# Cross-attention for 64 batches: one output projection and one sum of heads move to the end of a step

## The chip, the cores and the metric

The kernel runs on one core of one Trainium2 chip. The core has a matrix engine (PE, with its weight loads shown apart as PEld), a vector engine (DVE), an activation engine (ACT), a general engine (POOL) and a queue that issues transfers (SP). The metric is the time of one execution on the device, in microseconds (us); lower is better.

## The reference

For each of 64 batches there are 256 queries of width 320 and 77 context rows of width 512. Of these 69 are text and 8 belong to an image prompt, each with its own key and value weights. There are 20 heads of width 16. Text and image part have softmaxes of their own, and their results are added:

```
q = split_heads(x @ w_q)
out_text = sdpa(q, split_heads(text @ w_k), split_heads(text @ w_v))
out_ip   = sdpa(q, split_heads(ip @ w_k_ip), split_heads(ip @ w_v_ip), mask=box_mask)
out = (merge_heads(out_text) + merge_heads(out_ip)) @ w_out + b_out + x
```

`sdpa` is softmax(q k^T / 4 + mask) v. The mask of the image part comes from four boxes on a 16 x 16 grid of queries.

## The kernel before

A first part (to about 240 us) projects keys and values of all batches and stores them in device memory. The second part does the attention. It is a software pipeline over batches: step n works on batch a = n+1 (transposing x, projecting q, maxima of the scores), b = n (scores and exponentials), c = n-1 (sums over keys, output of queries 0 to 127) and d = n-2 (output of queries 128 to 255). All engines run the same steps. Four steps, then a hardware loop whose body holds six steps (so there is a loop-back every six steps), then the last steps.

Each step has 7 positions s = 0 to 6. Nothing reorders the work: every engine executes its instructions in the order in which its `step` function writes them, and the engines meet at semaphores. PE's order is at L963 to L993, ACT's at L999 to L1055, DVE's at L1066 to L1184, POOL's at L1190 to L1211. The work that matters here:

- `scores(b, s)`: matmuls of 2 of the 13 tiles of keys into one of three banks `ps_s`; ACT makes two exponentials of them, and POOL a remainder (`prob_lo`).
- `max_scores(a, m)`, m = 0 to 9, into two banks `ps_m`; DVE's `maxima(m)` adds the mask and reduces them into `stats` (L1097, L1100, and for m = 8 and 9 also L1104). max_scores(m) waits for maxima(m-2).
- `stats_transpose(a)` (L879): two PE transposes of `stats` into `ps_b`. It waits for the last reduction of maxima(9). ACT copies the result into `q_hi_extra` (L1052, and L1053 with four copies); the lower-half matmuls of the next step's scores (L905) need it. `x_transpose(a, 1)` waits for L1053 because it writes `ps_b`.
- `x_transpose(a, 0)` (L828): the first PE work of a step, into `ps_a`. Its wait on `s_yr` asks for the `finish(c, 0)` of the step before.
- `attn_transpose`, `project_out(c, 0)` (L951, a bias matmul L959 and 8 matmuls at L852 into `ps_a`), then DVE's `finish(c, 0)` (L1135), which adds x into `y`. SP stores `y`.
- `sum_heads(c, u)`, u = 0 to 5 (L909): matmuls of the probabilities with the spread values into the single bank `ps_o`. DVE's `invert(u)` (L1110) and `norm(u)` (L1118) empty it; POOL adds the two parts into `attn` (L1208). sum_heads(u) waits for norm(u-1). u = 5, a group of 4 heads, is the last.
- `spread_values` (L1145): three DVE multiplications at s = 4, 5, 6.
- At the start of the next step ACT and DVE split the transposed x (`x_hi`, `x_lo`), which `project(a, 0)` (PE, L852 into `ps_b`) waits for.

Of the kernel before, what the change touches and what calls it, by code (L numbers as in the profile page):

```python
# [37 lines left out]
UNITS = NT * 3  # L38
# [93 lines left out]
def xattn_kernel(nc, x, ctx, bbox, w_q, w_k, w_v, w_k_ip, w_v_ip, w_out, b_out,  # L132
# [6 lines left out]
    with ctx_stack:  # L139
# [513 lines left out]
        with ExitStack() as st:  # L653
# [99 lines left out]
            with nc.Block() as block:  # L753
# [71 lines left out]
                def _(pe):  # L825
# [53 lines left out]
                    def stats_transpose(b, n):  # L879
                        pe.wait_ge(s_ip, at(b, NT, NT))  # L880

                        if n is None or n >= 1:
                            pe.wait_ge(s_alo, at(b, NT, 1 - 2 * NT))
                        else:
                            pe.wait_ge(s_qlo, at(b, QUADS, 4))
                        for t in range(NT):
                            last = nc.tensor.transpose(ps_b[:, t * P:(t + 1) * P], stats[:, t, :], ident[:])  # L887
                        last.then_inc(s_et, 1)
# [62 lines left out]
                    def project_out(b, t, A):  # L951
                        pe.wait_ge(s_alo, at(b, NT, t + 1))

                        if t == 0 and A:
                            pe.wait_ge(s_qlo, at(b, QUADS, QUADS * 2 + 5))
                        elif t == 0:
                            wait(pe, s_yr, b, NT, 0)
                        c = slice(t * P, (t + 1) * P)
                        mm(ps_a[:, 0:D], ones[:], bias[:], start=True, stop=False)  # L959
                        split_product(ps_a[:, 0:D], lambda k: aT[0][:, k, c], lambda k: aT[1][:, k, c], aT2[:, c],  # L960
                                      wo, slice(0, D), False, False).then_inc(s_op, 1)

                    def step(pe, b, n):  # L963
                        A, Bs, Cs, Ds = has(n)
                        a, c = off(b, 1), off(b, -1)
                        d = off(b, -2)
                        for s in range(PAIRS):
                            if A and s == 0:
                                x_transpose(a, 0, n)
                            if Bs:  # L970
                                scores(b, s)
                            if A and s == 0:
                                x_transpose(a, 1, n)
                            if Ds and s == 1:
                                attn_transpose(d, 1, A, n)
                            if Ds and s == 2:
                                project_out(d, 1, A)
                            if A and s in (1, 2, 3):
                                project(a, s - 1)
                            if A and MAXIMA[s]:  # L980
                                max_scores(a, MAXIMA[s][0])
                            if Cs:
                                if s == 4:
                                    attn_transpose(c, 0, A, n)
                                if s == 5:
                                    project_out(c, 0, A)
                                if s < UNITS:
                                    sum_heads(c, s)
                            if A:
                                for m in MAXIMA[s][1:]:  # L990
                                    max_scores(a, m)
                        if A:
                            stats_transpose(a, n)  # L993

                    sched(pe, step)

                @block.scalar
# [62 lines left out]
                def _(dve):  # L1060
# [5 lines left out]
                    def step(dve, b, n):  # L1066
                        A, Bs, Cs, Ds = has(n)
# [59 lines left out]
                        def finish(c, t):  # L1127
                            dve.wait_ge(s_op, at(c, NT, t + 1))
                            if t == 0:
                                dve.wait_ge(s_xk[par(c)], nth(c, 16))  # L1130

                                reg = c[0] is not None
                                if reg or c[1] >= 2:
                                    dve.wait_ge(s_y[par(c)], nth(c, 32, -32))
                            nc.vector.tensor_tensor(y[par(c)][:, t, :], ps_a[:, 0:D], x_keep[par(c)][:, t, :],  # L1135
                                                    ALU.add).then_inc(s_yr, 1)

                        def spread_values(g):

                            if g == 0:  # L1140
                                dve.wait_ge(s_vals[par(b)], nth(b, 16 * NVDMA))
                                wait(dve, s_pv, b, UNITS, -UNITS)
                            v = values[par(b)][:].rearrange("p (t n c) -> p t n c", t=TILES, c=SLOT)
                            t = slice(GTILE[g], GTILE[g] + GTILES[g])
                            nc.vector.tensor_tensor(  # L1145
                                v[:, t, :, 2:SLOT],
                                raw_v[par(b)][:].rearrange("p t (o c) -> p t o c", o=1)[:, t]
                                .broadcast_to([P, GTILES[g], SLOTS, 3 * DH]),
                                own_rows[:].rearrange("p t (n c) -> p t n c", n=SLOTS)[:, t], ALU.mult).then_inc(s_vx, 1)
# [7 lines left out]
                        for s in range(PAIRS):  # L1157
                            if A and s == 0:
                                x_lo(0)
                                x_lo(1)  # L1160
                            if Ds and s == 1:
                                a_lo(d, 1)
                            if Ds and s == 2:
                                finish(d, 1)
                            if A and MAXIMA[s]:
                                maxima(MAXIMA[s][0])
                            if A and s in (1, 2, 3):
                                q_lo(s - 1)
                            if Cs and s == 4:
                                a_lo(c, 0)  # L1170
                            if Cs and s == 5:
                                finish(c, 0)
                            if Cs and s < UNITS:
                                invert(s)
                            if A:
                                for m in MAXIMA[s][1:2]:
                                    maxima(m)
                            if Cs and s < UNITS:
                                norm(s)
                            if A:  # L1180
                                for m in MAXIMA[s][2:]:
                                    maxima(m)
                            if Bs and s in (4, 5, 6):
                                spread_values(s - 4)  # L1184

                    sched(dve, step)

# [48 lines left out]
```

## Time and profile before

| What | Value |
|---|---|
| median of 3 runs (lowest, highest) | 1598.76 us (1596.06, 1602.39) |
| the profiled execution, its time | 1604.02 us |
| the profiled execution, its span in the trace | 1602.1 us |
| PE busy | 1385.2 us (86%) |
| PEld busy | 1266.7 us (79%) |
| DVE busy | 1173.1 us (73%) |
| ACT busy | 848.4 us (53%) |
| POOL busy | 806.3 us (50%) |
| mean granted PE clock | 0.959 |

The span covers one execution, from its first instruction to its last. Busy time is the time in which an engine executes; it says nothing of whether the others wait for it. The granted clock is 1.0 at 2.4 GHz and 0.5 at 1.2 GHz, the two levels at which PE runs.

### The profile page before, as it was taken

What the parts mean: (1) busy time and instruction counts of PE and PEld (TensorE: products, weight loads), DVE (VectorE), ACT (ScalarE), POOL (GpSimd) and SP (SyncE); (2) the same over time, 40 slices, a digit from 0 to 9 for tenths busy, and PEclk for the clock granted to TensorE, in tenths of its full rate; (3) what the DMA queues carried; (4) which work ended last, traced back from release to release, by engine and by line L of the source; (5) the groups of instructions that cost most, each with busy time, mean ns of one, the idle gap of its engine ahead of it and who ended that gap; (6) DMA issues with size and microseconds to landing.
All of it is one profiled execution on the core that took longest, in us unless ns stands there. A gap on an engine that the chain in (4) does not pass through costs nothing.

```text
span 1602.1 us, 48578 instructions
## 1 busy us (share of the span) xinstructions
PE 1385.2 (86%) x15736; PEld 1266.7 (79%) x15736; DVE 1173.1 (73%) x3602; ACT 848.4 (53%) x2064; POOL 806.3 (50%) x1038
## 2 busy tenths in 40 slices
PE   6778775899989989989998998998998998999997
PEld 5778774788878878878887887887887888888886
DVE  5368443788878877877887886887887886888885
ACT  3344432555555555555555555555554555555553
POOL 0132220555555555555555555555555555555554
PEclk9899995999999999999999999999999999999998
DMA  5788994343333443433433333433433333444331
GB/s 136 112 199 171 187 168 88 84 93 94 92 74 89 93 95 88 93 93 87 93 93 86 93 93 71 94 92 88 93 93 91 94 93 85 93 94 93 94 76 37
DMA packets 361215, 159.25 MB, mean 99 GB/s; under 512 B 298417, under 2 KB 350514, under 8 KB 359666
## 3 DMA queue, kind: packets, MB, share of 16 engines
q1 hardware_dynamic: 355826, 134.83, 37.3%
q10 hardware_dynamic: 5120, 20.98, 6.3%
q8 instruction: 152, 2.49, 0.7%
q14 instruction: 117, 0.96, 0.2%
HBM read 91.69 MB, written 43.05 MB: 84 GB/s over the span
## 4 chain that ended last, share of the span: by engine, by line
PE 42%; DVE 14%; issue 14%; ACT 10%; ACTq 2%; DVEq 1%; POOL 1%; DMA 0%; POOLq 0%; SPq 0%
PE ps_o L928 9%; PE ps_a L852 9%; PE ps_b L852 8%; PE ps_m L876 5%; PE ps_s L899 4%; PE ps_s L905 4%; ACT prob_hi L1037 3%; DVE values L1145 3%; ACT xT_hi L1007 2%; DVE y L1135 2%; PE ps_b L887 2%; DVE stats L1104 2%; ACT aT_hi L1025 2%; ACTq L1018 2%; DVE inv L1110 1%
## 5 line engine op out<-in xcount | busy, mean ns | idle before, releaser
L1197 POOL TENSOR_TENSOR prob_lo<-prob,prob_hi 128x512 f16<-128x512 f32 (+1 forms) x448 | 488.9, 1091 | 169.5 <-ACT prob_hi L1037 169.3
L1208 POOL TENSOR_TENSOR attn<-heads 128x128 f32<-128x128 f32 (+1 forms) x512 | 271.9, 541 | 440.0 <-DVE heads L1118 440.0
L1036 ACT ACTIVATE prob<-ps_s 128x512 f32<-128x512 f32 (+1 forms) x448 | 254.0, 567 | 388.6 <-PE ps_s L905 379.9
L928 PE MATMUL ps_o<-values,prob_hi 128*128 128x64 bf16 (+7 forms) x4992 | 311.3, 196 | 3.8 <-DVE values L1145 1.8
L928 PE MATMUL ps_o<-values,prob_lo 128*128 128x68 bf16 (+7 forms) x3328 | 300.2, 196 | 0.0
L928 PEld LDWEIGHTS ps_o<-values,prob_hi 128*128 128x128 f16 x4992 | 268.8, 99 | 25.8 <-DVE values L1145 2.0
L1100 DVE TENSOR_REDUCE stats<-ps_m 128x4 f32<-128x276 f32 x640 | 277.0, 433 | 0.0
L899 PE MATMUL ps_s<-q_hi_lo,keys 128*128 128x256 f32 x960 | 260.3, 305 | 0.0
L1037 ACT ACTIVATE prob_hi<-ps_s 128x512 f16<-128x512 f32 (+1 forms) x448 | 251.4, 561 | 0.0
L905 PE MATMUL ps_s<-q_hi_extra,keys 128*128 128x256 f32 x960 | 246.1, 292 | 0.9 <-ACT q_hi_extra L1052 0.3
L876 PE MATMUL ps_m<-keys,q_hi_lo 128*128 128x308 f32 x640 | 219.2, 360 | 12.7 <-DVE stats L1100 4.8
L928 PEld LDWEIGHTS ps_o<-values,prob_lo 128*128 128x128 f16 x3328 | 217.0, 99 | 0.0
L905 PEld LDWEIGHTS ps_s<-q_hi_extra,keys 128*128 128x128 f32 x960 | 177.6, 195 | 11.4 <-ACT q_hi_extra L1052 11.1
L899 PEld LDWEIGHTS ps_s<-q_hi_lo,keys 128*128 128x128 f32 x960 | 178.4, 196 | 0.0
L1118 DVE TENSOR_TENSOR heads<-ps_o,inv 128x256 f32<-128x256 f32 (+1 forms) x384 | 143.3, 373 | 15.1 <-DVE inv L1110 0.5
L876 PEld LDWEIGHTS ps_m<-keys,q_hi_lo 128*128 128x128 f32 x640 | 116.3, 190 | 41.4 <-DVE stats L1100 33.0
L1014 ACT CAST q_hi_lo<-ps_b 64x256 fp32r<-64x256 f32 x256 | 94.1, 368 | 100.7 <-PE ps_b L852 97.4
L1097 DVE TENSOR_TENSOR ip_masked<-ps_m,stats 128x32 f32<-128x32 f32 x640 | 105.1, 164 | 54.9 <-PE ps_m L876 48.8
L1145 DVE TENSOR_TENSOR values<-raw_v,own_rows 128x1200 bf16<-128x1200 bf16 (+1 forms) x192 | 136.3, 737 | 0.0
L1087 DVE TENSOR_TENSOR q_hi_lo<-ps_b,q_hi_lo 64x256 fp32r<-64x256 f32 x256 | 108.1, 422 | 14.9 <-ACT q_hi_lo L1014 7.0
L1110 DVE RECIPROCAL inv<-ps_o 128x16 f32<-128x16 f32 (+1 forms) x384 | 91.6, 239 | 15.3 <-PE ps_o L928 5.6
L852 PE MATMUL ps_b<-xT_hi,wq_hi 128*128 128x256 f32 x256 | 80.3, 314 | 17.3 <-DVE xT L1074 15.4
(165 smaller groups left out, 3032.5 us busy)
## 6 DMA issues: line engine op xcount, KB each, us to landing
x_in<-in_x_dram SPq DMA_DIRECT2D x64, 320.0 KB, 3.3
q_hi_extra<-q_hi_lo ACTq DMA_DIRECT2D x64, 320.0 KB, 3.3
x_keep<-in_x_dram SPq DMA_DIRECT2D x64, 320.0 KB, 3.2
out_dram<-y SPq DMA_DIRECT2D x128, 160.0 KB, 1.8
k_scratch<-k_stage SPq DMA_DIRECT2D x16, 770.0 KB, 5.8
keys<-k_scratch SPq DMA_DIRECT2D x256, 48.1 KB, 2.0
ctx_in<-in_ctx_dram SPq DMA_DIRECT2D x64, 128.0 KB, 3.1
v_scratch<-v_stage SPq DMA_DIRECT2D x64, 120.0 KB, 5.5
```

Source lines behind the costliest of these rows:

```text
L852: last = mm(ps, ww if swap else a, a if swap else ww, start=first and n == 0, stop=n == len(terms) - 1)
L876: mm(ps_m[n % 2][:, 0:QUAD], q_hl[par(b)][:, h4, t * P:(t + 1) * P], keys[:, third(b), 0, h4, KOFF:KOFF + QUAD], start=True, stop=True).th ...
L899: mm(ps, keys[:, n, 0, quad, c:c + P], q_hl[q][:, quad, :], start=i == 0, stop=False)
L905: last = mm(ps, keys[:, n, 1, quad, c:c + P], q_ex[q][:, quad, :], start=False, stop=i == len(QPARTS[t]) - 1)
L928: last = mm(o[:, :, oo:oo + w], stat, v[:, :, a:a + w], start=first, stop=False, skip_group_check=True)
L1036: nc.scalar.activation(prob[:, s, 0:w], ps_s[RING[s]][:, 0:w], ACT.Exp)
L1037: nc.scalar.activation(prob_hi[par(b)][:, s, 0:w], ps_s[RING[s]][:, 0:w], ACT.Exp).then_inc(s_hi, 1)
L1100: nc.vector.tensor_reduce(stats[:, t, R_MT + 4 * h4:R_MT + 4 * h4 + 4], ps[:, :, 0:T], AX.X, ALU.max).then_inc(s_mx, 1)
L1118: nc.vector.tensor_tensor(heads[u % 2][:, 0:ns, :], o[:, :, 1:17], inv[:, 0:ns].rearrange("p (n o) -> p n o", o=1).broadcast_to([P, ns, DH ...
L1145: nc.vector.tensor_tensor(v[:, t, :, 2:SLOT], raw_v[par(b)][:].rearrange("p t (o c) -> p t o c", o=1)[:, t] .broadcast_to([P, GTILES[g], S ...
L1197: nc.gpsimd.tensor_tensor(prob_lo[par(b)][:, s, 0:w], prob[:, s, 0:w], prob_hi[par(b)][:, s, 0:w], ALU.subtract).then_inc(s_lo, 1)
L1208: last = nc.gpsimd.tensor_tensor(attn[:, t, c0:c0 + nh * DH].rearrange("p (h c) -> p h c", c=DH), hv[:, :, 0, :], hv[:, :, 1, :], ALU.add)
```

## The change

The pieces `project_out(c, 0)` and `sum_heads(c, 5)` leave position 5 of a step on PE and stand behind `stats_transpose(a)`, at the very end of the step. DVE's matching pieces `finish(c, 0)`, `invert(5)` and `norm(5)` leave position 5 and stand behind the last `spread_values`. ACT, POOL and SP keep their orders. No instruction is added or left out.

```diff
--- before.py
+++ after.py
@@ -982,15 +982,16 @@
                             if Cs:
                                 if s == 4:
                                     attn_transpose(c, 0, A, n)
-                                if s == 5:
-                                    project_out(c, 0, A)
-                                if s < UNITS:
+                                if s < UNITS - 1:
                                     sum_heads(c, s)
                             if A:
                                 for m in MAXIMA[s][1:]:
                                     max_scores(a, m)
                         if A:
                             stats_transpose(a, n)
+                        if Cs:
+                            project_out(c, 0, A)
+                            sum_heads(c, UNITS - 1)
 
                     sched(pe, step)
 
@@ -1168,20 +1169,22 @@
                                 q_lo(s - 1)
                             if Cs and s == 4:
                                 a_lo(c, 0)
-                            if Cs and s == 5:
-                                finish(c, 0)
-                            if Cs and s < UNITS:
+                            if Cs and s < UNITS - 1:
                                 invert(s)
                             if A:
                                 for m in MAXIMA[s][1:2]:
                                     maxima(m)
-                            if Cs and s < UNITS:
+                            if Cs and s < UNITS - 1:
                                 norm(s)
                             if A:
                                 for m in MAXIMA[s][2:]:
                                     maxima(m)
                             if Bs and s in (4, 5, 6):
                                 spread_values(s - 4)
+                        if Cs:
+                            finish(c, 0)
+                            invert(UNITS - 1)
+                            norm(UNITS - 1)
 
                     sched(dve, step)
```

The changed file has one line more above its DVE part, so a DVE line of before has a number one higher there.

PE, where position 5 of one of the first steps ends (later steps have the same order): a `-` is a row of before, a `+` one of the changed order. `L876` is max_scores(9), `L899` and `L905` scores(6), `L887` stats_transpose, `L959` and the first `L852` the start of project_out(c, 0).

```order
 L899 MATMUL ps_s<-q_hi_lo,keys 128x256
 L905 MATMUL ps_s<-q_hi_extra,keys 128x256
-L876 MATMUL ps_m<-keys,q_hi_lo 128x308
+L876 MATMUL ps_m<-keys,q_hi_lo 128x308 x2
+L899 MATMUL ps_s<-q_hi_lo,keys 128x256
+L905 MATMUL ps_s<-q_hi_extra,keys 128x256
+L887 MATMUL ps_b<-ident,stats 128x128 x2
 L959 MATMUL ps_a<-bias,ones 128x320
 L852 MATMUL ps_a<-wo_hi,aT_hi 128x320
```

max_scores(9), scores(6) and the transposes of the statistics now come ahead of project_out. The other end of the same piece, behind the last matmuls of sum_heads(5) (`L928`), where the next step's x_transpose (`L841`) follows:

```order
 L928 MATMUL ps_o<-values,prob_lo 128x34
 L928 MATMUL ps_o<-values,prob_lo 128x2x16
-L876 MATMUL ps_m<-keys,q_hi_lo 128x308
-L899 MATMUL ps_s<-q_hi_lo,keys 128x256
-L905 MATMUL ps_s<-q_hi_extra,keys 128x256
-L887 MATMUL ps_b<-ident,stats 128x128 x2
 L841 MATMUL ps_a<-ident,x_in 128x128 x2
 L843 MATMUL ps_a<-ident,x_in 128x128
```

The next step's first transposes used to follow the transposes of the statistics, and now follow sum_heads(5).

DVE, from maxima(8) to the first instruction of the next step, before (`L1135` is finish, `L1110` invert, `L1118` norm, `L1145` spread_values, `L1154` the next step's copy of the mask):

```order
L1097 TENSOR_TENSOR ip_masked<-ps_m,stats 128x32
L1100 TENSOR_REDUCE stats<-ps_m 128x4
L1104 TENSOR_REDUCE stats<-ip_masked 128x20
L1135 TENSOR_TENSOR y<-ps_a,x_keep 128x320
L1110 RECIPROCAL inv<-ps_o 128x8
L1097 TENSOR_TENSOR ip_masked<-ps_m,stats 128x32
L1100 TENSOR_REDUCE stats<-ps_m 128x4
L1104 TENSOR_REDUCE stats<-ip_masked 128x20
L1118 TENSOR_TENSOR heads<-ps_o,inv 128x128
L1145 TENSOR_TENSOR values<-raw_v,own_rows 128x25x48
L1145 TENSOR_TENSOR values<-raw_v,own_rows 128x15x48
L1154 COPY stats<-mask 128x2x8
```

And the same stretch as changed (line numbers one higher):

```order
L1098 TENSOR_TENSOR ip_masked<-ps_m,stats 128x32
L1101 TENSOR_REDUCE stats<-ps_m 128x4
L1105 TENSOR_REDUCE stats<-ip_masked 128x20
L1098 TENSOR_TENSOR ip_masked<-ps_m,stats 128x32
L1101 TENSOR_REDUCE stats<-ps_m 128x4
L1105 TENSOR_REDUCE stats<-ip_masked 128x20
L1146 TENSOR_TENSOR values<-raw_v,own_rows 128x25x48
L1146 TENSOR_TENSOR values<-raw_v,own_rows 128x15x48
L1136 TENSOR_TENSOR y<-ps_a,x_keep 128x320
L1111 RECIPROCAL inv<-ps_o 128x8
L1119 TENSOR_TENSOR heads<-ps_o,inv 128x128
L1155 COPY stats<-mask 128x2x8
```

maxima(9) now follows maxima(8) directly, and finish, invert and norm stand behind both spreads.

## Rows read from the trace of the kernel before

**Rows 1.** Stretches, all engines: us, busy us per engine, PEclk, DMA share, GB/s

```profile
1031.00:1051.00 20.00, 18.27 (x226) 16.63 (x226) 16.26 (x54) 11.82 (x29) 11.71 (x15) 1.00 0.40 93
...
1091.00:1116.50 25.50, 20.67 (x226) 19.12 (x226) 16.26 (x55) 11.81 (x29) 11.76 (x15) 0.87 0.32 76
```

**Rows 2.** Waits: engine, line, releaser: us in total, times, longest us

```profile
PE ps_b L887 <- DVE stats L1104: 67.2, 64, 2.1
...
PE ps_a L841 <- issue: 28.2, 8, 3.9
...
DVE stats L1154 <- issue: 11.1, 8, 1.6
```

**Rows 3.** PE, timeline, one step's end: start, us, what [idle before <- releaser]

```profile
1007.71 0.41 PE L959 MATMUL ps_a<-bias,ones 128*128 128x320 f32 x1
...
1009.14 0.25 PE L928 MATMUL ps_o<-values,prob_hi 128*128 128x51 bf16 x3
...
1009.60 0.39 PE L876 MATMUL ps_m<-keys,q_hi_lo 128*128 128x308 f32 x1
1009.83 0.28 PE L899 MATMUL ps_s<-q_hi_lo,keys 128*128 128x256 f32 x1
1009.95 0.28 PE L905 MATMUL ps_s<-q_hi_extra,keys 128*128 128x256 f32 x1
1011.24 0.44 PE L887 MATMUL ps_b<-ident,stats 128*128 128x128 f32 x2 [1.01 <-DVE stats L1104]
1011.51 0.38 PE L841 MATMUL ps_a<-ident,x_in 128*128 128x128 f32 x2
...
1011.76 0.36 PE L899 MATMUL ps_s<-q_hi_lo,keys 128*128 128x256 f32 x1
...
1013.05 0.44 PE L841 MATMUL ps_b<-ident,x_in 128*128 128x128 f32 x2 [0.29 <-ACT q_hi_extra L1053]
...
1015.24 0.27 PE L949 MATMUL ps_a<-ident,attn 128*128 128x128 f32 x1
1015.77 0.39 PE L852 MATMUL ps_b<-xT_hi,wq_hi 128*128 128x256 f32 x1 [0.25 <-DVE xT L1074]
```

**Rows 4.** DVE, timeline, the same step's end

```profile
1007.91 0.43 DVE L1100 TENSOR_REDUCE stats<-ps_m 128x4 f32<-128x276 f32 x1
...
1009.96 0.48 DVE L1135 TENSOR_TENSOR y<-ps_a,x_keep 128x320 f32<-128x320 f32 x1
...
1010.47 0.13 DVE L1097 TENSOR_TENSOR ip_masked<-ps_m,stats 128x32 f32<-128x32 f32 x1
...
1010.88 0.30 DVE L1104 TENSOR_REDUCE stats<-ip_masked 128x20 f32<-128x160 f32 x1
1011.10 0.28 DVE L1118 TENSOR_TENSOR heads<-ps_o,inv 128x128 f32<-128x128 f32 x1
1011.30 1.34 DVE L1145 TENSOR_TENSOR values<-raw_v,own_rows 128x1200 bf16<-128x1200 bf16 x2
```

**Rows 5.** ACT, timeline, just behind it

```profile
1013.02 0.37 ACT L1007 CAST xT_hi<-ps_a 128x256 fp32r<-128x256 f32 x1
...
1013.45 0.60 ACT L1036 ACTIVATE prob<-ps_s 128x512 f32<-128x512 f32 x1
```

**Rows 6.** POOL, timeline, the two adds of the last sum

```profile
1011.46 1.36 POOL L1208 TENSOR_TENSOR attn<-heads 128x64 f32<-128x64 f32 x2 [0.67 <-DVE heads L1118]
```

**Rows 7.** PE, timeline behind a loop-back

```profile
1095.02 0.69 PE L841 MATMUL ps_a<-ident,x_in 128*128 128x128 f32 x2 [3.43 <-issue]
...
1100.83 0.50 PE L852 MATMUL ps_b<-xT_hi,wq_hi 128*128 128x256 f32 x1
```

**Rows 8.** PE, timeline: first and last of six idle stretches of 1.6 to 2.1 us

```profile
93.89 0.87 PE L464 MATMUL ps_t<-ident,ctx_in 128*128 128x128 f32 x4 [1.81 <-DMA ctx_in<-in_ctx_dram]
...
1582.04 0.25 PE L928 MATMUL ps_o<-values,prob_hi 128*128 128x51 bf16 x3 [1.79 <-DVE values L1145]
```

**Rows 9.** Stretch behind the last of them, columns as in rows 1

```profile
1582.00:1586.00 4.00, 3.68 (x54) 3.31 (x55) 1.41 (x5) 0.53 (x2) 1.25 (x3) 0.57 0.02 4
```

## The prediction

> **What bounds the kernel now.** I read the time by stretches first, then the waits, then the timelines of one step. A step in the loop takes 20.0 us with PE busy for 18.3 of them at the full clock, and a step behind a loop-back takes 25.5 us, with a mean granted clock of 0.87 [rows 1]. PE is the busiest engine, so the question is where it is not busy. The list of waits answers: in each of 64 steps PE waits for DVE's last reduction before the transposes of the statistics, 67.2 us in all or 1.05 us each, and at each of 8 loop-backs it waits 3.5 us for nothing that the profile shows [rows 2]. The timeline of one step adds two short waits: 0.29 us until ACT has read `ps_b` empty, and 0.25 us for xT_lo [rows 3]. Call the start of the statistics' transposes T (1011.24 in the rows). Two chains meet there:
>
> - Up to T the end is set by DVE. From 1007.91 its rows follow each other without a gap: maxima, norm, a spread, maxima(8), y, an inversion, maxima(9) [rows 4]. PE is through with scores(6) at 1010.23 and stands still until T [rows 3].
> - From T to the first matmul of project(a, 0) at 1015.77 are 4.53 us. Here ACT is in line: it copies the statistics, then x_hi(0) from 1013.02, the exponentials from 1013.45, x_hi(1), and DVE's x_lo(1); from the exponentials' start to project are 2.32 us [rows 3, 5].
>
> From project to scores(4) of the step PE has work without a stop, and the change touches nothing there.
>
> **The change part by part.** Nothing is added or removed; three things move. I place them on the rows of the same step.
>
> *DVE ahead of T.* y, the inversion and their gaps stand between maxima(8) and maxima(9): 1010.47 - 1009.96 = 0.51 us [rows 4]. They go, so maxima(9) ends 0.51 us earlier and T comes at 1010.73. What is late next is the same chain of DVE.
>
> *PE ahead of T.* The moved matmuls last 1009.14 - 1007.71 = 1.43 us (project_out) and 1009.60 - 1009.14 = 0.46 us (sum_heads(5)), together 1.89 us [rows 3]. They ran while DVE worked towards T, so there they cost nothing. Without them PE has max_scores(9), which must wait for maxima(7) (its row ends at 1008.34 [rows 4]), then scores(6), and is done by about 1009.0. It then waits until 1010.73. The wait of 1.0 us becomes 1.7 us, with a new one of about 0.55 us shortly ahead of it. That is the heart of the forecast: PE had cover to give under DVE's chain, and the change takes it away.
>
> *Behind T.* The 1.89 us now stand between the transposes (0.27) and the next step. The two matmul groups hide ACT's copies, so the 0.29 us wait goes, and a wait of 0.2 us in the first scores. But x_transpose(0) may not start before y is made. project_out ends at T + 1.70, its last result 0.2 later; DVE has finished both spreads (1.34 us [rows 4]) by then and waits for it; y takes 0.48; so x_transpose(0) starts at T + 2.44, not at T + 2.16. Its three transposes reach ACT 0.49 later, x_hi(0) takes 0.43 until the exponentials can start [rows 5], which is T + 3.40; scores(0), four matmuls 0.12 apart [rows 3], is ready just before. With 2.32 more, project starts at T + 5.72. PE alone needs, from T + 2.44, 0.25 for the transposes, 0.5 for scores(0), and 1015.51 - 1013.05 = 2.46 for x_transpose(1) up to the end of attn_transpose [rows 3]: T + 5.65. Both limits are nearly equal. The stretch is 5.72 instead of 4.53 us: +1.19.
>
> *What is queued behind.* On DVE the inversion, norm(5) and the next step's mask copy stand behind y; they end by T + 3.2, before x_lo(0) can start. POOL's two adds, 1.36 us at most [rows 6], wait for norm(5) and then hold up one prob_lo; attn is ready at about T + 4.4, and attn_transpose comes at T + 5.0: hidden. SP stores y some 3 us later (y ends at T + 2.4, and at T - 0.8 before [rows 4]) and loads values behind it, for a step that is two away: hidden. If these covers fail the price is up to 1 us a step.
>
> *Sum at the full clock:* -0.51 + 1.19 = +0.68 us a step. 62 steps have both moved pieces and a next step, 8 of them end in a loop-back, so 54 x 0.68 = +37 us.
>
> *The clock.* This is the unknown. PE's longer stall may cost it the clock. In this trace there are six idle stretches of PE between 1.6 and 2.1 us that began at full clock, and behind four of them the clock fell; the last was 1.79 us long and the mean clock of the next 4 us was 0.57 [rows 8, 9]. At half clock for a time z in these 4 us the mean is 1 - z/8, so the low lasted about 3.4 us. The waits of 1.0 us in the steady steps never brought it down: the clock there is 1.00 [rows 1]. The new stall of 1.7 us, with 0.55 us of idleness near it, lies in the range of the six. Price of one fall: behind the loop-back the stretch from x_transpose(0) to project took 1100.83 - 1095.02 = 5.81 us at half clock [rows 7], against 0.25 + 0.5 + 2.46 = 3.2 us, so work runs 1.8 times as long; 3.4 us of it put PE back by 1.5 us, of which the small waits above take 0.2: 1.3 us. Bounds: 0 where it never falls, 1.3 a step where it falls in each. By the rows, 4 of 6; the second idle stretch close by speaks for more; I take three in four, 0.98 us a step: 54 x 0.98 = +53 us.
>
> The Trainium skill speaks against this. "TensorE: Matmul & The Clock Gate", section "Why this matters for your kernels", asks only that idle gaps between bursts of matmuls stay below a length that is well above the stall that I expect. By that rule the clock would hold and the sum would be that of the first rival. The trace does not agree: a gap of 1.79 us was enough at 1582.
>
> *The loop-back.* In 8 steps the stall of 3.5 us came straight behind T's transposes and hid ACT's work. If it starts only when the moved work is done, such a step grows by 1.89 - 0.51 = 1.4 us; if PE's queue takes the moved matmuls while the next code is fetched, it shrinks by 0.5 at best, less what is left: -0.3. DVE's rows speak for overlap: at the same loop-backs DVE, with 1.34 us of spreads in its queue, stood idle for only 1.4 us where PE stood 3.5 [rows 2, 4]. I take +0.6: 8 x 0.6 = +5 us. The clock is low behind loop-backs anyway.
>
> The skill's table at the head of the same page gives TensorE a queue of 64 instructions, into which the 24 moved matmuls and their weight loads would fit; by that the lower end holds and the sum is 7 us less. No row shows PE's queue at a loop-back with work in it.
>
> **Sum.** 37 + 53 + 5 = +95 us on the profiled execution's own time of 1604.0 us (its span is 1602.1): 1699 us. The median of the runs shown, 1598.8, is 5.3 lower, so I forecast 1694 us.
>
> **The rivals.**
>
> *The clock holds.* Then 37 + 5 = +42 us: 1641 us. For it: 20.0 us steps with a 1.0 us wait and further small ones keep the full clock, and two of the six gaps did no harm, one of them 2.04 us long. Against: the other four.
>
> *The clock falls in every step.* 54 x (0.68 + 1.3) + 8 x 1.4 = +118 us: 1717 us. It is the upper part of my own case.
>
> *Faster: T moves further ahead than I place it.* If DVE reached maxima(9) earlier than 1010.73, because its work before T shortens when PE and POOL press less on it, the moved matmuls would fill waits that are worth 1.0 + 0.29 + 0.2 + 0.25 us. It decides at T = 1010.05, where the step's length is unchanged. At T = 1009.5 the step gains 0.55 us: 54 x 0.55 = -30 us: 1569 us. Against it: DVE's rows before T have no gap to give back, and the only instructions removed from them are those 0.51 us.
>
> *No effect.* The new waits replace the old ones one for one, 1599 us. It would need T near 1010.05 as well.
>
> **How the numbers follow.** The clock falls in most steps: 0.58, and this is the forecast, with a range of its own of 1665 to 1722. The clock holds: 0.27. Some mixture or a hidden cost between the other cases, slower by more than 0.5%: 0.04. No effect within 0.5% (8 us, about what a measurement of this kernel can tell from no change): 0.04. Faster: 0.07. So faster 0.07, same 0.04, slower 0.89. The range has to take in the rival with the clock held, with some room below (1630), and the case of a fall in each step above (1725).
>
> **What would show it.** In the changed profile: (1) PE's wait before L887 on DVE's L1105 grows from 1.05 to about 1.7 us a step, and waits before the max_scores on DVE's L1101 grow by about 0.5 us a step; (2) ACT's L1053 no longer releases PE; x_transpose(0) waits for DVE's y (L1136) for some tenths; (3) from T to the first matmul of project are about 5.7 us in a step at full clock; (4) the mean granted clock of the span falls from 0.96 to about 0.92 (three quarters of 54 lows of 3.4 us at half clock in 1699 us are 0.04), with lows inside steady steps and not only behind loop-backs; (5) steady steps of 20.7 us where the clock holds and near 22 where it falls. I am wrong if T comes ahead of 1010.05 on the scale of these rows, or if PE's stall before T isn't longer than before; the clock term alone is wrong if lows stay confined to the loop-backs.

## The result, and the profile after

| | before | changed |
|---|---|---|
| median of 4 runs (lowest, highest) | 1598.8 us (1596.06, 1602.39) | 1685.13 us (1683.01, 1690.06) |
| profiled execution, span | 1602.1 us | 1681.2 us |
| mean granted PE clock over the span | 0.959 | 0.934 |

The changed kernel is slower: the ratio of its time to that of before is 1.054, 95% interval 1.051 to 1.057. The forecast was 1694 us with a range of 1630 to 1725.

The page of the changed kernel, first part and clock row (tenths of full speed in 40 slices), and below them the clock row of before. The work is the same, but low slices now stand all over the span:

```profile
PE 1405.9 (84%) x15736; PEld 1298.2 (77%) x15736; DVE 1179.0 (70%) x3602; ACT 851.0 (51%) x2064; POOL 759.2 (45%) x1038
...
PEclk9889977999999989989899998998998998989998
```

```profile
PEclk9899995999999999999999999999999999999998
```

Three stretches of the changed kernel, each one step long, columns as in [rows 1]: a step at full clock, a step with a fall of the clock, a step with a loop-back.

```profile
449.31:470.11 20.80, 18.04 (x227) 16.57 (x227) 16.30 (x54) 11.88 (x29) 10.95 (x16) 1.00 0.38 90
1470.81:1492.76 21.95, 19.43 (x226) 17.93 (x227) 16.33 (x54) 11.92 (x29) 10.94 (x16) 0.91 0.36 85
603.72:630.14 26.42, 21.34 (x226) 19.89 (x227) 16.55 (x54) 11.82 (x29) 11.01 (x16) 0.81 0.32 74
```

A plain step takes 20.8 us where it took 20.0, and the step at 1470.81 holds a clock fall far from any loop-back (mean 0.91); between 300 us and the last T no step of before held one, apart from those with a loop-back. The loop-back's step takes 26.4 us at a mean clock of 0.81, against 25.5 and 0.87 [rows 1].

The waits of the changed kernel that answer [rows 2], with two new ones (us in total, times, longest us):

```profile
PE ps_b L887 <- DVE stats L1105: 112.7, 64, 2.1
...
PE ps_m L876 <- DVE stats L1101: 39.0, 77, 0.7
...
DVE stats L1155 <- issue: 24.0, 8, 3.2
...
PE ps_a L841 <- issue: 22.2, 8, 3.7
...
PE ps_a L841 <- DVE y L1136: 10.7, 38, 0.4
```

PE's wait before the statistics' transposes has grown from 67.2 to 112.7 us, it now waits for maxima ahead of max_scores (39.0 us, 4.8 before) and for y ahead of the next x_transpose (10.7 us). At the loop-backs PE's wait has shrunk, from 28.2 to 22.2 us, and DVE's has grown from 11.1 to 24.0.

PE's timeline at one step's end, the answer to [rows 3]. T, the start of L887, is here 407.72:

```profile
405.34 0.41 PE L876 MATMUL ps_m<-keys,q_hi_lo 128*128 128x308 f32 x1 [0.56 <-DVE stats L1101]
...
407.72 0.44 PE L887 MATMUL ps_b<-ident,stats 128*128 128x128 f32 x2 [1.74 <-DVE stats L1105]
407.91 0.39 PE L959 MATMUL ps_a<-bias,ones 128*128 128x320 f32 x1
...
409.32 0.25 PE L928 MATMUL ps_o<-values,prob_hi 128*128 128x51 bf16 x3
...
410.15 0.41 PE L841 MATMUL ps_a<-ident,x_in 128*128 128x128 f32 x2 [0.21 <-DVE y L1136]
...
413.51 0.39 PE L852 MATMUL ps_b<-xT_hi,wq_hi 128*128 128x256 f32 x1
```

DVE in the same place, the answer to [rows 4] (numbers one higher: L1098, L1105 maxima, L1146 spreads, L1136 y):

```profile
406.23 0.18 DVE L1098 TENSOR_TENSOR ip_masked<-ps_m,stats 128x32 f32<-128x32 f32 x1
...
407.35 0.31 DVE L1105 TENSOR_REDUCE stats<-ip_masked 128x20 f32<-128x160 f32 x1
407.58 1.24 DVE L1146 TENSOR_TENSOR values<-raw_v,own_rows 128x1200 bf16<-128x1200 bf16 x2
409.51 0.49 DVE L1136 TENSOR_TENSOR y<-ps_a,x_keep 128x320 f32<-128x320 f32 x1 [0.69 <-PE ps_a L852]
```

And ACT behind T, the answer to [rows 5]:

```profile
408.46 1.01 ACT L1054 CAST q_hi_extra<-ps_b 64x1024 fp32r<-64x1024 f32 x1
...
411.20 0.60 ACT L1037 ACTIVATE prob<-ps_s 128x512 f32<-128x512 f32 x1
```

From the first row on DVE to the end of L1105 are 1.43 us, and PE stands idle for 0.56 and 1.74 us ahead of T. Behind it the moved matmuls fill 407.91 to 409.8, x_transpose(0) starts at T + 2.43, the exponentials at T + 3.48, project at T + 5.79.

To see where the 79.1 us between the two spans are, I take a step from one start of L887 to the next, and call a step full if the granted clock never leaves its upper level in it (steps from 300 us on):

| | before | changed | difference in all |
|---|---|---|---|
| steps between loop-backs, full | 53 x 19.98 us | 35 x 20.84 us | 53 x 0.86 = +45.8 |
| steps with a fall | none | 18 x 22.10 us | 18 x 1.26 = +22.7 |
| steps with a loop-back | 8 x 25.09 us | 8 x 26.50 us | +11.3 |
| the first two steps | 39.9 us | 37.0 us | -2.9 |
| ahead of the first T, behind the last | 302.7 us | 305.0 us | +2.3 |

### The profile page after: what moved, and what is told of

The parts are those of the page before. It is cut to its first block, busy times and chain, and to the rows that moved or that the text cites. A ratio compares the mean times of both kernels' runs of the same rounds, so it can differ in the third digit from the quotient of the medians.

```text
span 1681.2 us, 48569 instructions
## 1 busy us (share of the span) xinstructions
PE 1405.9 (84%) x15736; PEld 1298.2 (77%) x15736; DVE 1179.0 (70%) x3602; ACT 851.0 (51%) x2064; POOL 759.2 (45%) x1038
## 4 chain that ended last, share of the span: by engine, by line
PE 49%; DVE 13%; issue 12%; ACT 7%; ACTq 2%; POOL 1%; DVEq 0%; DMA 0%; POOLq 0%; SPq 0%
PE ps_a L852 13%; PE ps_o L928 9%; PE ps_b L852 8%; PE ps_m L876 5%; PE ps_s L899 4%; PE ps_s L905 4%; ACT prob_hi L1038 3%; DVE values L1146 3%; DVE stats L1105 2%; PE ps_b L887 2%; PE ps_a L841 2%; ACTq L1019 1%; ACT aT_hi L1026 1%; DVE y L1136 1%; DVE stats L1101 1%
## 5 line engine op out<-in xcount | busy, mean ns | idle before, releaser
L1211 POOL TENSOR_TENSOR attn<-heads 128x128 f32<-128x128 f32 (+1 forms) x512 | 223.7, 447 | 609.3 <-DVE heads L1119 609.3
L928 PE MATMUL ps_o<-values,prob_hi 128*128 128x64 bf16 (+7 forms) x4992 | 317.7, 198 | 4.7 <-DVE heads L1119 4.7
L928 PE MATMUL ps_o<-values,prob_lo 128*128 128x68 bf16 (+7 forms) x3328 | 304.7, 198 | 0.0
L928 PEld LDWEIGHTS ps_o<-values,prob_hi 128*128 128x128 f16 x4992 | 275.4, 100 | 28.0 <-issue 8.0
L899 PE MATMUL ps_s<-q_hi_lo,keys 128*128 128x256 f32 x960 | 261.6, 308 | 0.0
L876 PE MATMUL ps_m<-keys,q_hi_lo 128*128 128x308 f32 x640 | 219.7, 360 | 47.3 <-DVE stats L1101 39.0
L905 PE MATMUL ps_s<-q_hi_extra,keys 128*128 128x256 f32 x960 | 243.4, 289 | 0.0
L928 PEld LDWEIGHTS ps_o<-values,prob_lo 128*128 128x128 f16 x3328 | 219.9, 100 | 0.0
L876 PEld LDWEIGHTS ps_m<-keys,q_hi_lo 128*128 128x128 f32 x640 | 115.8, 189 | 89.8 <-DVE stats L1101 81.4
L899 PEld LDWEIGHTS ps_s<-q_hi_lo,keys 128*128 128x128 f32 x960 | 181.2, 199 | 0.0
L905 PEld LDWEIGHTS ps_s<-q_hi_extra,keys 128*128 128x128 f32 x960 | 180.8, 198 | 0.0
L1098 DVE TENSOR_TENSOR ip_masked<-ps_m,stats 128x32 f32<-128x32 f32 x640 | 108.1, 169 | 53.2 <-PE ps_m L876 47.5
L1146 DVE TENSOR_TENSOR values<-raw_v,own_rows 128x1200 bf16<-128x1200 bf16 (+1 forms) x192 | 130.9, 708 | 0.0
L1136 DVE TENSOR_TENSOR y<-ps_a,x_keep 128x320 f32<-128x320 f32 x128 | 62.9, 492 | 92.0 <-PE ps_a L852 91.8
L887 PE MATMUL ps_b<-ident,stats 128*128 128x128 f32 x128 | 30.0, 319 | 112.7 <-DVE stats L1105 112.7
```

Of the source, the lines that this page charges most:

```text
L876: mm(ps_m[n % 2][:, 0:QUAD], q_hl[par(b)][:, h4, t * P:(t + 1) * P], keys[:, third(b), 0, h4, KOFF:KOFF + QUAD], start=True, stop=True).th ...
L899: mm(ps, keys[:, n, 0, quad, c:c + P], q_hl[q][:, quad, :], start=i == 0, stop=False)
L905: last = mm(ps, keys[:, n, 1, quad, c:c + P], q_ex[q][:, quad, :], start=False, stop=i == len(QPARTS[t]) - 1)
L928: last = mm(o[:, :, oo:oo + w], stat, v[:, :, a:a + w], start=first, stop=False, skip_group_check=True)
L1146: nc.vector.tensor_tensor(v[:, t, :, 2:SLOT], raw_v[par(b)][:].rearrange("p t (o c) -> p t o c", o=1)[:, t] .broadcast_to([P, GTILES[g], S ...
L1211: last = nc.gpsimd.tensor_tensor(attn[:, t, c0:c0 + nh * DH].rearrange("p (h c) -> p h c", c=DH), hv[:, :, 0, :], hv[:, :, 1, :], ALU.add)
```

## The experiments

Nine kernels ran; every time is compared with runs of the kernel before on the same chip. "Full step" is the mean over the steps described above, T the start of the statistics' transposes.

| kernel | median, us | ratio (95%) | full step, us | stall at T, us | T to project, us | steps with a fall, of 53 |
|---|---|---|---|---|---|---|
| before | 1598.8 | 1 | 19.98 | 1.01 | 4.53 | 0 |
| changed | 1685.1 | 1.054 (1.051 to 1.057) | 20.84 | 1.73 | 5.86 | 18 |
| 1 projection alone | 1687.7 | 1.056 (1.054 to 1.059) | 20.90 | 1.03 | 5.79 | 21 |
| 2 last sum alone | 1596.8 | 0.999 (0.998 to 1.001) | 19.91 | 1.50 | 4.53 | 0 |
| 3 DVE's order alone | 1579.2 | 0.987 (0.984 to 0.990) | 19.59 | 0.63 | 4.53 | 0 |
| 4 changed, filled stall | 1671.1 | 1.045 (1.043 to 1.047) | 20.84 | 0.57 | 5.86 | 0 |
| 5 changed, early spread | 1626.6 | 1.015 (1.009 to 1.021) | 20.14 | 1.04 | 5.86 | 10 |
| 6 as 3, early spread | 1573.7 | 0.983 (0.981 to 0.985) | 19.59 | 0.63 | 4.53 | 0 |
| 7 as 6, last sum behind T | 1541.4 | 0.963 (0.961 to 0.965) | 19.04 | 0.63 | 4.53 | 0 |
| 8 as 7, max_scores(9) first | 1568.2 | 0.981 (0.979 to 0.983) | 19.36 | 0 | 4.93 | 0 |
| 9 as 7, spread late | 1578.2 | 0.987 (0.985 to 0.989) | 19.51 | 1.09 | 4.53 | 0 |

Stall and T to project are medians over the full steps, and falls are counted in one profiled execution of each kernel. They vary from execution to execution: the four of kernel 5 lie between 1614 and 1634 us, with mean clocks from 0.957 down to 0.939.

An edit moves the line numbers below it. The last reduction of maxima, L1104 of before, is L1105 in the changed kernel and in kernel 5, L1106 in kernels 2, 7 and 9, and L1109 in kernel 4; in kernel 8 all of these numbers are four higher than before.

### 1. The projection alone behind the transposes

Against the changed kernel, PE part; on DVE inversion and norm of the last sum are back at position 5 likewise, finish stays at the end:

```diff
-                                if s < UNITS - 1:
+                                if s < UNITS:
                                     sum_heads(c, s)
...
                             project_out(c, 0, A)
-                            sum_heads(c, UNITS - 1)
```

Expected:

> Only the output projection and DVE's finish stand behind the transposes of the statistics; the last sum of heads with its inversion and norm stays at position 5. Theory (PE's cover under DVE's chain is lost, and the way transposes -> projection -> y -> next x_transpose sets the rest): the projection carries nearly all of the loss. T moves 0.4 us ahead (y's share of the 0.51), the stretch from T to project stays near 5.8 us, full-clock steps 20.7 to 20.9 us, some falls of the clock in steady steps: 1665 to 1690 us. Rival (the single bank ps_o and norm(5) in front of the next sum_heads(0) cause the loss): with the last sum back in its place the step is near 20.1 us and the time 1600 to 1615 us.

Measured: 1687.7 us, as slow as both moves together. One step of PE's timeline:

```profile
410.28 0.25 PE L928 MATMUL ps_o<-values,prob_hi 128*128 128x51 bf16 x3 [0.90 <-DVE heads L1118]
...
412.39 0.44 PE L887 MATMUL ps_b<-ident,stats 128*128 128x128 f32 x2 [1.02 <-DVE stats L1104]
...
414.84 0.41 PE L841 MATMUL ps_a<-ident,x_in 128*128 128x128 f32 x2 [0.68 <-DVE y L1135]
...
418.18 0.38 PE L852 MATMUL ps_b<-xT_hi,wq_hi 128*128 128x256 f32 x1
```

From T to project are 5.79 us. The theory holds and the rival falls: the projection carries the loss. T lies behind a different pair of waits than in the changed kernel: without the projection in between, sum_heads(5) has to wait 0.90 us for norm(4) (`ps_o` is one bank), and 1.02 us are left at T. That is 1.9 us of idleness ahead of T against 2.3 in the changed kernel, and the clock falls as often.

The equal totals are in part chance. The full steps are alike (20.90 and 20.84 us), but the 21 steps with a fall take 22.96 us here, 2.06 us more than a full one where a fall cost 1.26 us in the changed kernel (the clock is low for 5.8 us of such a step, there for 3.8 us), and the steps with a loop-back take 24.5 us instead of 26.5.

### 2. The last sum alone behind the transposes

```diff
+                                if s == 5:
+                                    project_out(c, 0, A)
                                 if s < UNITS - 1:
                                     sum_heads(c, s)
...
-                            project_out(c, 0, A)
                             sum_heads(c, UNITS - 1)
```

(and on DVE finish is back at position 5.)

Expected:

> Only the last sum of heads, its inversion and norm stand behind the transposes; projection and finish stay at position 5. Theory: the next x_transpose then starts 0.46 us after its old place, which ACT's copies of 1.8 us hide, so T to project stays near 4.55 us; T moves by 0.1 us at most; PE's stall before T is about 1.3 us. Step 19.9 to 20.1 us, no falls of the clock in steady steps: 1590 to 1606 us. Rival (ps_o and norm(5) cause the loss): about the changed kernel's 20.8 us a step, 1650 us or more.

Measured: 1596.8 us, ratio 0.999. PE's timeline:

```profile
402.02 0.44 PE L887 MATMUL ps_b<-ident,stats 128*128 128x128 f32 x2 [1.49 <-DVE stats L1106]
...
402.75 0.42 PE L841 MATMUL ps_a<-ident,x_in 128*128 128x128 f32 x2
...
406.55 0.39 PE L852 MATMUL ps_b<-xT_hi,wq_hi 128*128 128x256 f32 x1 [0.25 <-DVE xT L1076]
```

x_transpose(0) starts at T + 0.73 instead of T + 0.27, and project still at T + 4.53: ACT's copies hide the 0.46 us. What PE loses ahead of T comes back as a longer stall, 1.49 us. So the length of the stall at T by itself costs nothing; it is the same end of DVE's chain seen from a PE that arrives earlier. And it did not bring the clock down in one of 53 steps, though it is only 0.2 us shorter than the changed kernel's.

### 3. DVE's order alone

Against the kernel before; PE's order is untouched.

```diff
-                            if Cs and s == 5:
-                                finish(c, 0)
-                            if Cs and s < UNITS:
+                            if Cs and s < UNITS - 1:
                                 invert(s)
...
-                            if Cs and s < UNITS:
+                            if Cs and s < UNITS - 1:
+                                norm(s)
+                            if Cs and s == 5:
+                                finish(c, 0)
+                                invert(s)
                                 norm(s)
```

Expected:

> PE's order is that of before; on DVE finish, inversion and norm of the last sum stand behind maxima(9), ahead of the two spreads. Theory (DVE's chain alone sets T): T comes 0.5 us earlier and PE's wait there shrinks from 1.0 to 0.5 us; x_transpose(0) waits for y about 0.2 us, hidden by ACT's copies; the spreads end 0.5 to 0.9 us later against T, so sum_heads(0) may wait some tenths. Step 19.5 to 19.8 us: 1570 to 1590 us, faster than both kernels. Rival (PE's own work, or ACT, sets the end of the step, and DVE's order does not matter): 1595 to 1602 us.

Measured: 1579.2 us, ratio 0.987: faster than both. DVE's timeline at one T, and PE's rows of that T and the next:

```profile
400.05 0.31 DVE L1104 TENSOR_REDUCE stats<-ip_masked 128x20 f32<-128x160 f32 x1
400.27 0.48 DVE L1135 TENSOR_TENSOR y<-ps_a,x_keep 128x320 f32<-128x320 f32 x1
400.67 0.20 DVE L1110 RECIPROCAL inv<-ps_o 128x8 f32<-128x8 f32 x1
400.97 0.29 DVE L1118 TENSOR_TENSOR heads<-ps_o,inv 128x128 f32<-128x128 f32 x1
```

```profile
400.41 0.44 PE L887 MATMUL ps_b<-ident,stats 128*128 128x128 f32 x2 [0.63 <-DVE stats L1104]
...
419.99 0.44 PE L887 MATMUL ps_b<-ident,stats 128*128 128x128 f32 x2 [0.63 <-DVE stats L1104]
```

y now runs while PE makes the transposes, and a step is 19.58 us long. The gain is 0.39 us a step where 0.51 were taken out of DVE's chain: the stall could not shrink below 0.63 us, which experiments 6 and 8 take up.

### 4. The changed kernel with work in PE's stall

```diff
+                        if A and Cs:
+                            pe.wait_ge(s_qlo, at(c, QUADS, QUADS * 2 + 5))
+                            for _ in range(8):
+                                mm(ps_a[:, 0:D], ones[:], bias[:], start=True, stop=True)
                         if A:
                             stats_transpose(a, n)
```

Expected:

> The changed kernel with 8 further matmuls (ones by bias, into ps_a, whose result the projection overwrites; 8 x 0.147 = 1.2 us) between scores(6) and the transposes of the statistics, where PE stands idle for 1.73 us. Theory (the falls in steady steps come from that idleness and cost 1.26 us each, and T is DVE's): T does not move, full-clock steps stay at 20.84 us, no lows in steady steps; the 18 falls x 1.26 = 23 us go: 1655 to 1670 us. Rival 1 (T depends on PE): the step grows by up to 1.2 us, 1740 us or more. Rival 2 (the falls have another cause): lows in steady steps stay, about 1685 us.

Measured: 1671.1 us, just above the expected 1655 to 1670. PE's rows of two successive T, and the long stretch (columns as in [rows 1]; the lows left in it are those at the loop-backs):

```profile
408.39 0.44 PE L887 MATMUL ps_b<-ident,stats 128*128 128x128 f32 x2 [0.57 <-DVE stats L1109]
...
429.15 0.44 PE L887 MATMUL ps_b<-ident,stats 128*128 128x128 f32 x2 [0.56 <-DVE stats L1109]
```

```profile
306.00:1600.00 1294.00, 1158.63 (x13919) 1067.92 (x13919) 967.59 (x3146) 706.80 (x1726) 652.27 (x893) 0.98 0.37 86
```

The two T lie 20.76 us apart, as in the changed kernel; over all full steps both have 20.84. So PE's 1.2 us of extra work is free, T is not PE's, and the falls were caused by the idleness: 18 steps of 22.10 have become steps of 20.84. That is the 22.7 us of the table above; between the two spans the kernel gained only 11.4 us, since its steps with a loop-back take 27.8 us instead of 26.5, and its first two steps 2.2 us more. The expectation left the loop-backs as they were. Kernel 4's waits show where they grew:

```profile
PE ps_a L841 <- issue: 22.9, 8, 3.1
PE ps_b L841 <- issue: 15.0, 8, 2.3
```

The first wait is that of the changed kernel (22.2 us). The second, ahead of x_transpose(1), is new: 1.9 us at each loop-back in which PE again waits for nothing that the profile shows. Why the further instructions bring it is not shown.

### 5. The changed kernel with a spread out of DVE's chain

```diff
-                            if Bs and s in (4, 5, 6):
-                                spread_values(s - 4)
+                            if Bs and s in (1, 5, 6):
+                                spread_values(s // 5 + s // 6)
```

Expected:

> The changed kernel with spread_values(0) of a step moved from position 4, ahead of T, to the end of position 1, where DVE stands idle for some tenths. Theory (in the changed kernel T is set by DVE's chain alone, PE having been ready 1.73 us earlier): T comes about 0.7 us earlier, the stall falls to about 1.0 us, T to project stays at 5.8 us, full-clock steps 20.1 us, few or no falls in steady steps: 1600 to 1620 us, so most of the loss goes without touching PE's order. Rival (the step's length is set by PE's longer serial part behind T and by ps_o): steps stay at 20.8 us, 1680 us or so.

Measured: 1626.6 us, ratio 1.015. PE's two waits ahead of one T:

```profile
406.61 0.41 PE L876 MATMUL ps_m<-keys,q_hi_lo 128*128 128x308 f32 x1 [0.56 <-DVE stats L1101]
...
408.30 0.44 PE L887 MATMUL ps_b<-ident,stats 128*128 128x128 f32 x2 [1.05 <-DVE stats L1105]
```

The full step fell by 0.70 us, about the length of one spread (two of them take 1.34 us in [rows 4]), while PE's order and T to project (5.86) stayed. That bears out the theory: in the changed kernel the 0.70 us taken off DVE ahead of T came off the step whole. The time lies somewhat above the expected 1600 to 1620 because 10 steps still had a fall.

### 6. The same spread moved in kernel 3

The edit is that of experiment 5, on kernel 3. Expected:

> PE as before; DVE with finish, inversion and norm behind maxima(9) and spread_values(0) at the end of position 1. Theory: T can come at most 0.63 us earlier than with the DVE order alone, since PE's stall there is 0.63 us; then PE sets T. Steps 18.95 to 19.1 us: 1540 to 1555 us. Rival (something other than DVE's work ahead of T, such as ACT's exponentials of position 4, holds T): 1570 to 1582 us.

Measured: 1573.7 us, a full step of 19.59 us as in kernel 3. The expectation of 1540 to 1555 us failed, and the rival was nearer, though for another reason. PE's row at T, and DVE's first instruction of maxima(9):

```profile
418.01 0.44 PE L887 MATMUL ps_b<-ident,stats 128*128 128x128 f32 x2 [0.63 <-DVE stats L1104]
```

```profile
417.19 0.19 DVE L1097 TENSOR_TENSOR ip_masked<-ps_m,stats 128x32 f32<-128x32 f32 x1 [0.69 <-PE ps_m L876]
```

The stall is 0.63 us to the hundredth in kernels 3, 6 and 7. DVE no longer sets T by its backlog: here it stands idle for 0.69 us until max_scores(9) is done. What is left is the way from PE's max_scores(9) through DVE's three instructions back to PE, less the time of scores(6), which stands in between. It moves only if max_scores(9) is issued earlier. What is won against kernel 3 (7.1 us between the two spans) lies in the first two steps (2.2 us), the loop-backs (2.2 us), and ahead of the first T and behind the last (2.6 us together).

### 7. Kernel 6 with the last sum behind T

```diff
-                                if s < UNITS:
+                                if s < UNITS - 1:
                                     sum_heads(c, s)
...
                             stats_transpose(a, n)
+                        if Cs:
+                            sum_heads(c, UNITS - 1)
```

(on DVE inversion and norm of the last sum stand at the end of the step, finish stays behind maxima(9).)

Expected:

> As the kernel with both moves on DVE, and the last sum of heads (0.46 us on PE) behind the transposes of the statistics, its inversion and norm at the end of DVE's step. Theory: once PE sets T, the 0.46 us are hidden behind T by ACT's copies (1.8 us), so the step shrinks by 0 to 0.4 us more, as far as DVE's chain lets it: 1520 to 1550 us. Rival (the sum costs the same wherever it stands): as the kernel with both moves alone.

Measured: 1541.4 us, ratio 0.963: the fastest kernel of the study. PE's rows of two successive T:

```profile
399.49 0.44 PE L887 MATMUL ps_b<-ident,stats 128*128 128x128 f32 x2 [0.63 <-DVE stats L1106]
...
418.55 0.44 PE L887 MATMUL ps_b<-ident,stats 128*128 128x128 f32 x2 [0.63 <-DVE stats L1106]
```

A step is 19.06 us here. The 0.46 us of the last sum no longer stand ahead of max_scores(9), so the way through DVE begins earlier by that much, and behind T they are hidden as in experiment 2. The other 0.09 us are mostly in that way itself: from the start of max_scores(9) to T are 1.17 us (398.32 to 399.49), and 1.25 in kernel 6. The time lies in the expected range partly by luck: I had expected 0 to 0.4 us off the step of a kernel of 1540 to 1555 us, and it was 0.55 us off one of 1573.7. This is half of the change under study, and it pays 0.55 us a step once DVE is not late.

### 8. Kernel 7 with max_scores(9) ahead of the projection

```diff
                                 if s == 5:
+                                    if A:
+                                        max_scores(a, MAXIMA[s][1])
                                     project_out(c, 0, A)
```

Expected:

> The kernel with both moves on DVE and the last sum behind T, and PE's max_scores(9) ahead of project_out at position 5. Theory: the stall of 0.63 us before T that stayed the same in three kernels is the time from max_scores(9) through DVE's three instructions back to PE, less scores(6); with 1.4 us of projection in between it goes, until DVE's chain sets T again. Steps 18.7 to 18.95 us: 1520 to 1538 us. Rival (the 0.63 us are DVE's chain from earlier in the step): steps stay at 19.04 us, 1541 us.

Measured: 1568.2 us, slower than kernel 7. PE's and ACT's timelines near T = 416.46:

```profile
414.65 0.41 PE L876 MATMUL ps_m<-keys,q_hi_lo 128*128 128x308 f32 x1 [0.54 <-DVE stats L1104]
414.90 0.31 PE L959 MATMUL ps_a<-bias,ones 128*128 128x320 f32 x1
...
416.46 0.38 PE L887 MATMUL ps_b<-ident,stats 128*128 128x128 f32 x2
...
418.68 0.44 PE L841 MATMUL ps_b<-ident,x_in 128*128 128x128 f32 x2 [0.30 <-ACT q_hi_extra L1057]
```

```profile
416.67 0.38 ACT L1040 ACTIVATE prob<-ps_s 128x256 f32<-128x256 f32 x1 [1.57 <-PE ps_s L905]
...
417.62 1.01 ACT L1057 CAST q_hi_extra<-ps_b 64x1024 fp32r<-64x1024 f32 x1
```

The stall at T is gone, so the reading of the 0.63 us was right. But max_scores(9) now waits 0.54 us for maxima(7), and scores(6) ends just ahead of T, so that ACT's last exponentials (416.67) run behind T and push its copies of the statistics back: x_transpose(1) starts at T + 2.22 instead of T + 1.81. The account is -0.63 + 0.54 + 0.40 = +0.31 us; measured 19.36 - 19.04 = +0.32. My number was wrong because it left out both.

### 9. Kernel 7 with the spread back at position 4

The edit of experiment 5 is undone. Expected:

> The kernel with DVE's finish behind maxima(9) and the last sum of heads, inversion and norm behind T, but spread_values(0) back at position 4. Theory: with 0.46 us less on PE ahead of T, DVE's chain with the spread in it (0.7 us) sets T again: steps 19.4 to 19.6 us, 1570 to 1580 us, about the DVE order alone. Rival (what is on DVE ahead of T no longer matters once finish is out of it): 19.04 us a step as with the early spread, 1541 us.

Measured: 1578.2 us, a full step of 19.51 us, as expected. PE's row at T:

```profile
405.10 0.44 PE L887 MATMUL ps_b<-ident,stats 128*128 128x128 f32 x2 [1.09 <-DVE stats L1106]
```

With the spread ahead of T DVE is the late one again, and the last sum behind T gains only 0.08 us over kernel 3. The pieces interact: each move pays only as far as the other engine is not the late one.

## Why the prediction was right, and where its sizes were off

- **DVE sets T, and T comes 0.51 us earlier.** Right, with 0.47 us measured. From maxima(8)'s first instruction to the end of the last reduction there are now 1.43 us (406.23 to 407.66 in DVE's rows), where by the rows of before y and the inversion stood in between. The step's length outside T to project fell by 0.47 us (20.84 - 5.86 against 19.98 - 4.53). Experiments 3, 4 and 5 show that DVE is the cause.
- **PE loses its cover.** Right in size: 1.73 us at T (forecast 1.7) and 0.56 us ahead of max_scores(9) (forecast 0.55).
- **Behind T.** Right: x_transpose(0) waits for y and starts at T + 2.43 (forecast T + 2.44); project starts at T + 5.79 in the step shown, 5.86 in the median (forecast 5.72; its terms up to the exponentials add up to T + 3.36 and not to the T + 3.40 written there, and T + 3.48 was measured). Experiments 1 and 2 show that it is the projection, by way of y, and not the last sum. The sum of both parts was +0.68 a step and measured +0.86; 53 x 0.18 = 10 us of the error are here.
- **The clock.** The mechanism was right, its size not. A fall costs 1.26 us (forecast 1.3), but falls came in 18 of 53 steps, not in three of four: +23 us where the sum had +53. The mean clock of the span is 0.934, forecast 0.92. The step that failed is the step from "four of six" idle stretches to a share of the steps. The stalls are alike in all 53, so their length does not decide alone.
- **The loop-back.** +1.4 us each, forecast +0.6; that is the figure of the case without overlap (1.89 - 0.51). T to project grew by 1.9 us there, from 9.1 to 11.1 us in the mean, and the rest of the step fell by 0.5. PE's wait did fall by 0.75 us (28.2 to 22.2 us over 8), but mostly where the moved matmuls run at a low clock and so last longer. In six of the eight loop-backs the clock falls about 0.9 us behind T, while they run, and the wait is 2.2 to 2.8 us; in the other two it holds until T + 4.7 at least, and PE waits 3.75 and 3.28 us, as long as before (3.2 to 3.9 us). One of each kind:

```profile
476.07 0.68 PE L841 MATMUL ps_a<-ident,x_in 128*128 128x128 f32 x2 [3.75 <-issue]
...
609.20 0.69 PE L841 MATMUL ps_a<-ident,x_in 128*128 128x128 f32 x2 [2.33 <-issue]
```

What failed is the overlap that the sum counted on: the moved 1.89 us stand in T to project in full. The early fall (mean clock 0.81 instead of 0.87 [rows 1] in the step shown), which the sum left out as well, is not what makes up the difference: the wait takes up most of it, and the six steps with it last 26.3 to 26.7 us, the other two 25.7 and 26.9. DVE, which now has no spreads left in its queue at that point, waits 3.0 us instead of 1.4.
- **Together:** terms of 37, 53 and 5 us stand against 46, 23 and 11. The forecast +95 us met +86 between the medians and +79 between the two spans shown (the profiled execution of before was the slowest of its four, that of the changed kernel the fastest). The total was near by luck: errors of opposite sign met. The first rival (the clock holds, 1641 us) was refuted by the falls; what experiment 4 makes of it, a changed kernel without falls in plain steps, still took 1671 us, 30 more than that rival, mostly because its loop-backs cost 2.7 us each over before, and the full steps 0.18 us more than the sum had.
- **Hidden pieces.** POOL's adds and SP's store behind the moved norm cost nothing visible: PE waited on POOL a single time (1.4 us), as before.

## What to carry to other kernels

Moving work off the place just ahead of a wait shortens nothing if another engine's chain ends that wait: first ask which engine is late there, and shorten that one (here three DVE instructions, 1.3% alone). Work placed behind the wait is free only up to what the next engine in line hides (0.46 us were, 1.89 us with a result that the next step needs were not). And a move can pay after another has made its engine the late one: the last sum behind T gained next to nothing alone (0.07 us a step), and 0.55 us a step in kernel 7.

## What the runs showed of the hardware

- Two waits close to each other brought PE's clock down where a longer single one did not. A single stall of 1.49 us in each step gave no fall in 53 steps (kernel 2); 0.56 and then 1.05 us gave 10 (kernel 5), 0.56 and 1.73 us gave 18 (changed), 0.90 and 1.03 us with 0.68 behind T gave 21 (kernel 1). With 0.55 and 0.57 us there was none (kernel 4). The sum of the waits from max_scores(9) to project orders these kernels as well: about 1.4 us in kernel 4, 1.6 before and 1.8 in kernel 2, all without a fall, against 1.9 in kernel 5, 2.6 in the changed kernel and 2.7 in kernel 1. So the runs don't tell whether it is the pair or the sum that counts. None of these waits is as long as the idle gap that the Trainium skill warns of ("TensorE: Matmul & The Clock Gate", section "Why this matters for your kernels"): the runs do not agree with a rule on single gaps alone.
- Each such fall cost 1.26 us of a step in the changed kernel and 2.06 us in kernel 1, and filling the stall with matmuls that nobody reads removed them all and left the length of a full step as it was.
- At a loop-back DVE's wait, for which the profile names nothing, overlaps in part with work already queued: it was 1.4 us before and 2.0 us in kernels 3 and 6, where 1.34 us of spreads come last in DVE's order, and 2.8 to 3.1 us in the eight others, where y or the norm of the last sum comes last, both behind waits for PE.
